# Other orders on VectorE, ScalarE and GpSimd in a fused attention and mixture-of-experts kernel, with weight pieces in other slots and four zero products

## What is computed

```python
# x (4, 512, 512), ctx (4, 512, 128), all float32
# 1. sparse attention map from the context, added to the normalised x
Q = (h @ Wq.T).reshape(b, n, H, d).transpose(0, 2, 1, 3)
K = (h @ Wk.T).reshape(b, n, H, d).transpose(0, 2, 1, 3)
sim = jnp.einsum('bhnd,bhmd->bnm', Q, K) / (jnp.sqrt(jnp.float32(d)) * H)
threshold = jax.lax.top_k(sim, max(1, int(n * 0.3)))[0][:, :, -1:]     # the 153rd largest of each row
A_learned = jax.nn.sigmoid(sim) * (sim >= threshold)
A_learned = (A_learned + jnp.swapaxes(A_learned, -1, -2)) * 0.5
x = x + jnp.tanh(g_xattn[0]) * ((1.0 - gamma) * layernorm(x) + gamma * A_learned)
# 2. shared expert and two of eight routed experts on the normalised rows xf (2048, 512)
y, g = jnp.split(xf @ shared_gw.T, 2, axis=-1)                          # 2 x 704
shared = jax.nn.silu(g) * y @ shared_dw.T
scores = jax.nn.sigmoid(xf @ gate_w.T)
_, topk_idx = jax.lax.top_k(scores + gate_bias, 2)
w = jnp.take_along_axis(scores, topk_idx, axis=-1); w = w / jnp.sum(w, axis=-1, keepdims=True)
for e in range(8):                                                      # 2 x 352 hidden per expert
    g_e, u_e = jnp.split(xf @ up_w[e].T, 2, axis=-1)
    out = out + (jax.nn.silu(g_e) * u_e) @ down_w[e].T * we[:, None]
x = x + jnp.tanh(g_ffn[0]) * (shared + out)
```

## Time and profile before

| what | us |
|---|---|
| median of 3 runs (538.72 to 540.26) | 539.08 |
| the profiled execution | 540.25 |
| its span, first to last instruction | 538.4 |
| TensorE busy | 488.7 |
| VectorE busy | 328.4 |
| ScalarE busy | 254.3 |
| GpSimd busy | 219.9 |

### The profile page before, as it was taken

One profiled execution on the slowest core, in us unless ns is written; L12 is line 12 of the kernel. 1 busy time (PEld: TensorE's weight loads), 2 busy tenths in 40 slices (PEclk: granted clock), 3 DMA queues, 4 the chain that ended last, 5 costly groups with the idle time before them and its releaser, 6 DMA issues.

```text
span 538.4 us, 10344 instructions
## 1 busy us (share of the span) xinstructions
PE 488.7 (91%) x2992; PEld 266.9 (50%) x2993; DVE 328.4 (61%) x721; ACT 254.3 (47%) x465; POOL 219.9 (41%) x229
## 2 busy tenths in 40 slices
PE   7467988999898997999899999999999999999991
PEld 2234433544344443454446666666656656565650
DVE  2999897899868995689976773333323332323330
ACT  3874696889388946531315562222222222222220
POOL 2023367606773396302331443334443334444322
PEclk9758798999999998999999999999999999999997
DMA  5430333354435441330076986655665655566533
GB/s 197 153 103 2 120 103 84 84 179 141 124 83 174 147 110 35 138 103 2 0 271 196 244 213 115 121 101 97 107 102 105 114 108 97 99 110 106 105 40 39
DMA packets 45477, 61.57 MB, mean 114 GB/s; under 512 B 20544, under 2 KB 20800, under 8 KB 45440
## 3 DMA queue, kind: packets, MB, share of 16 engines
q1 hardware_dynamic: 36272, 40.53, 25.0%
q0 software_dynamic: 8736, 20.45, 22.0%
q10 hardware_dynamic: 432, 0.13, 0.1%
HBM read 37.90 MB, written 19.14 MB: 106 GB/s over the span
## 4 chain that ended last, share of the span: by engine, by line
PE 47%; DVE 32%; issue 8%; ACT 5%; DMA 3%; POOL 2%; DVEq 0%; ACTq 0%; POOLq 0%
PE py L1140 13%; PE pg L1120 12%; PE pu L1121 12%; DVE w L1238 5%; DMA out<-rows,idx 3%; PE pa L1130 2%; DVE work L1406 2%; PE pt_bank L896 2%; DVE pa L1268 2%; DVE w L1295 2%; DVE w L1285 2%; DVE w L1217 2%; DVE w L1603 1%; DVE w L1272 1%; ACT w L675 1%
## 5 line engine op out<-in xcount | busy, mean ns | idle before, releaser
L1120 PE MATMUL pg<-w,x_t 128*128 x408 | 123.3, 313 | 0.2
L1121 PE MATMUL pu<-w,x_t 128*128 x408 | 123.3, 313 | 0.0
L578 POOL DMA_INDIRECT out<-rows,idx x39 | 61.8, 1585 | 139.4 <-ACT rows L829 116.8
L962 PE MATMUL pg<-w 128*128 128x512 f16 x288 | 81.5, 402 | 6.0 <-DVE work L1406 6.0
L1140 PE MATMUL py<-w,work 128*128 x351 | 82.1, 379 | 0.8 <-DVE work L1666 0.8
L819 ACT ACTIVATE work<-pg 128x352 f32<-128x352 f32 x39 | 18.0, 463 | 125.5 <-PE pu L1121 125.3
L514 POOL TENSOR_TENSOR w<-stage,w 128x544 f16<-128x544 f32 x42 | 54.2, 1301 | 37.3 <-ACT stage L624 30.2
L962 PE MATMUL pu<-w 128*128 128x512 f16 x240 | 66.7, 388 | 0.0
L620 ACT ACTIVATE w<-stage 128x544 f16<-128x544 f32 x80 | 50.9, 648 | 26.9 <-DMA stage<-in_weights 26.3
L1666 DVE COPY work<-pa 128x768 f16<-128x768 f16 x39 | 21.8, 558 | 61.2 <-PE pa L1130 61.1
L1655 DVE SCALAR_TENSOR_TENSOR work<-pu,work 128x352 f32<-128x352 f32 x39 | 20.5, 525 | 62.7 <-ACT work L819 62.6
(11 more groups left out here) (245 smaller groups left out, 781.7 us busy)
## 6 DMA issues: line engine op xcount, KB each, us to landing
stage<-in_weights SPq DMA_DIRECT2D x80, 272.0 KB, 3.1
xn_rows<-w SPq DMA_DIRECT2D x16, 256.0 KB, 2.8
out<-w SPq DMA_DIRECT2D x16, 256.0 KB, 2.4
w<-in_x SPq DMA_DIRECT2D x3, 1024.0 KB, 5.3
w<-in_ctx_t SPq DMA_DIRECT2D x4, 256.0 KB, 3.9
w<-in_x SPq DMA_DIRECT2D x2, 512.0 KB, 3.7
out<-rows,idx POOLq DMA_INDIRECT x39, 4.9
work<-xn_rows,idx POOLq DMA_INDIRECT x20, 4.5
```

The source lines that it names most:

```text
L578: pool.indirect_dma_start(out=out, out_offset=bass.IndirectOffsetOnAxis(ap=idx[:, t:t + 1], axis=0), in_=rows[:, t % 2, :], in_offset=None ...
L962: mm = pe.matmul(bank_[:, :], w[:, half, part, at:at + P], x_tb[:, xpart * KC + k, :], start=(k, part, xpart) == (0, 0, 0), stop=(k, part) ...
L1120: pe.matmul(pg[p][:, 0:H], lhs, w[:, item, half, at:at + H], start=begin, stop=end)
L1121: mm = pe.matmul(pu[p][:, 0:H], lhs, w[:, item, half, at + H:at + 2 * H], start=begin, stop=end)
```

## The change

The line numbers of the kernel after are one to six higher.

1. `SLOT_PIECES` moves weight pieces: period 0 from (2, 2, 2, 2, 2, 3) to (2, 3, 3, 0, 0, 5), period 1 from (3, 3, 2, 0, 3, 3) to (4, 2, 2, 0, 1, 5), period 2 from (3, 3, 2, 0, 3, 2) to (4, 2, 2, 0, 1, 4). The periods keep their 13, 14 and 13 pieces.
2. GpSimd: `base_scalars` moves from slot 1 to slot 2 in periods 1 and 2; in the last slot all pieces but two come before the first `row_scalars`.
3. ScalarE: in period 0 the four `scaled_sigmoid` come before the first `count`; `keep_qk` comes after the third piece of the last slot, where it came after the first.
4. TensorE: four products with zeros stand between the second and the third turn of batch 0.
5. VectorE in period 0: `thresholds(0, 1)` before `shared_hidden(1)`, `shared_hidden(2)` before `thresholds(2, 3)`, `shared_hidden(3)` before `count_missed`.
6. VectorE in periods 1 and 2: `shared_hidden(3)` between the second and third mask.
7. VectorE in the router stage: `hot_slots(4)` and `(5)` after the hidden rows of their group, `tile_experts` from group 4 to after all eight steps and the first shared rows; the table follows it, and the shared rows of tile 1 stand between low pieces.

```diff
--- before.py
+++ after.py
@@ -23,7 +23,7 @@
 GATE_SCALE, PART_SCALE = 2.0 ** 14, 2.0 ** 11
 BY_PE = 6
 FIRST = 8
-SLOT_PIECES = ((2, 2, 2, 2, 2, 3), (3, 3, 2, 0, 3, 3), (3, 3, 2, 0, 3, 2))
+SLOT_PIECES = ((2, 3, 3, 0, 0, 5), (4, 2, 2, 0, 1, 5), (4, 2, 2, 0, 1, 4))
 KEEP = int(SEQ * 0.3)
 UP_W = KC * 2 * H
 ITEM_W = UP_W + JC * C
@@ -57,6 +57,7 @@
 WARM = 11
 WARM_FIRST = 7
 WARM_BETWEEN = 2
+WARM_TURN = 4
 
 
 def shared_at(flat):
@@ -540,7 +541,7 @@
 
             def together(b, more):
                 for u in range(UPS):
-                    if u == (1 if b else 0):
+                    if u == (2 if b else 0):
                         base_scalars(b + 1)
                     if (u or b) and u < TPB - 1:
                         for piece in slot_pieces(b, u):
@@ -552,12 +553,12 @@
                             for piece in slot_pieces(b, u):
                                 low_piece(*piece)
                 last = slot_pieces(b, UPS - 1)
-                low_piece(*last[0])
+                for piece in last[:-2]:
+                    low_piece(*piece)
                 row_scalars(b + 1, 0)
-                low_piece(*last[1])
+                low_piece(*last[-2])
                 row_scalars(b + 1, 1)
-                for piece in last[2:]:
-                    low_piece(*piece)
+                low_piece(*last[-1])
                 if more:
                     guess(b + 2)
                 o.clear()
@@ -753,8 +754,8 @@
             first_rows()
 
             def together(b, more):
-                count(b + 1, 0)
                 if b:
+                    count(b + 1, 0)
                     rows_turned(b, 3)
                     for n in range(1, ROUNDS):
                         count(b + 1, n)
@@ -762,6 +763,9 @@
                     scaled_sigmoid(b + 1, TPB - 1)
                     keep_logits(b)
                 else:
+                    for i in range(TPB):
+                        scaled_sigmoid(b + 1, i)
+                    count(b + 1, 0)
                     keep_logits(b)
                     count(b + 1, 1)
                     count(b + 1, 2)
@@ -770,17 +774,14 @@
                     if b == 0:
                         if u == 0:
                             count(b + 1, 3)
-                        if u in (1, 2):
-                            scaled_sigmoid(b + 1, 2 * u - 2)
-                            scaled_sigmoid(b + 1, 2 * u - 1)
                     pieces = slot_pieces(b, u)
                     ahead = {0: len(pieces) if b else 0, TPB: 0, UPS - 1: 1}.get(u, len(pieces))
                     for piece in pieces[:ahead]:
                         high_piece(*piece)
                     shared_high(b, u)
-                    if u == UPS - 1 and more:
-                        keep_qk(b + 2)
-                    for piece in pieces[ahead:]:
+                    for n, piece in enumerate(pieces[ahead:]):
+                        if u == UPS - 1 and more and n == 2:
+                            keep_qk(b + 2)
                         high_piece(*piece)
                 scores_and_rows(b + 1, more)
 
@@ -1003,8 +1004,12 @@
             project(1, None)
             for i in range(TPB):
                 scores(1, i)
-            for i in range(TPB):
-                turn_batch(0, i)
+            turn_batch(0, 0)
+            turn_batch(0, 1)
+            for n in range(WARM_TURN):
+                pe.matmul(py[:, :], zeros[:, 0:P], zeros[:, 0:512], start=True, stop=True)
+            turn_batch(0, 2)
+            turn_batch(0, 3)
             pe.wait_ge(gw_ok, 1)
 
             def together(b, more):
@@ -1459,8 +1464,9 @@
                     thresholds(b + 1, (2, 3))
                     shared_hidden(b, 2)
                     count_missed()
-                    masks(b + 1, range(TPB))
+                    masks(b + 1, (0, 1))
                     shared_hidden(b, 3)
+                    masks(b + 1, (2, 3))
                     check(b + 1)
                     shared_hidden(b, 4)
                     shared_hidden(b, 5)
@@ -1468,13 +1474,13 @@
                     shared_hidden(b, 0)
                     search(b + 1, 3)
                     last_counts(b + 1, (0, 1))
+                    thresholds(b + 1, (0, 1))
                     shared_hidden(b, 1)
-                    thresholds(b + 1, (0, 1))
                     last_counts(b + 1, (2, 3))
+                    shared_hidden(b, 2)
                     thresholds(b + 1, (2, 3))
-                    shared_hidden(b, 2)
+                    shared_hidden(b, 3)
                     count_missed()
-                    shared_hidden(b, 3)
                     masks(b + 1, (0, 1))
                     shared_hidden(b, 4)
                     masks(b + 1, (2, 3))
@@ -1632,20 +1638,18 @@
                 if u == 3:
                     hot_slots(2)
                     hot_slots(3)
-                if u == 4:
-                    hot_slots(4)
-                    tile_experts(ends)
-                if u == 5:
-                    hot_slots(5)
                 shared_hidden(BATCHES - 1, u)
+                if u >= 4:
+                    hot_slots(u)
             for step in range(HOTS, SLOTS_STEPS):
                 hot_slots(step)
+            shared_rows(BATCHES - 1, 0)
+            tile_experts(ends)
             table()
-            for n in range(RING):
+            for n in range(2):
                 low_piece(LATE, n)
-            shared_rows(BATCHES - 1, 0)
             shared_rows(BATCHES - 1, 1)
-            for n in range(RING, CHUNKS - 2):
+            for n in range(2, CHUNKS - 2):
                 low_piece(LATE, n)
 
 
```

## The result

The kernel after takes 540.96 us (median of 20 runs, 539.03 to 544.17), the kernel before in the same rounds 539.18 (20 runs, 538.09 to 541.76). The ratio is 1.0035, with a 95% interval of 1.0021 to 1.0049: **slower by 1.8 us**, where 0.8 us less had been forecast. Its profiled execution took 541.73 us, with a span of 539.9.

A forecast was written before the change was run, and what follows sets the result against it. TensorE was busy 488.7 of 538.4 us, leaving idle and half-speed time to win, though its waits were not the whole bound. Periods +1.6, -0.3, -2.6 and router stage +0.5 summed to -0.8 us: 538.3 us forecast, range 533.5 to 542.0.

## What to carry to other kernels

When a step is made later, follow every queue behind it to its last member, not only the first consumer: here the indices' first consumer lost nothing against before, and the price stood several queues on, at a wait for stores that before had just been met (landed by about 285.6 us, asked for at 286.24). A wait that no profile shows, because it was met in time, is a term of the sum: ask by how much it was met. On an engine whose serial work sets a result, moving a step within that work gained nothing here; idle time, added steps and the lengths that steps have beside another engine's work did count, and each order that served TensorE sooner bought that with idle time. And a wait on TensorE is worth removing only if what stands next is early too.
